# First column kept raw and gated during the forward half; last products of a column scan in two widths, last column stored in four pieces

## The reference

```
x = x + conv0(_gn(x));  x = x + conv1(_gn(x));  x = x + conv2(_gn(x))
# layer 3, on v = _gn(x), column by column (Wc is 1024 x 1024):
def step(prev, x_i):
    y = einsum('oc,nch->noh', Wc, prev) + conv_b
    y = where(y >= 0, y, prelu_a * y)
    return y + x_i
fl  = scan(step, v[..., 0], v[..., 1:])      # forward
out = scan(step, fl[31], fl[30 .. 0])        # back; the last column stays
x = x + out
```

## Time and profile before

| | us |
|---|---|
| median of 3 runs | 910.0 (908.2 to 911.15) |
| the profiled execution | 909.22 |
| its span, first to last instruction | 907.5 |
| TensorE busy | 780.0 (86%) |
| VectorE busy | 688.7 (76%) |
| ScalarE busy | 433.8 (48%) |
| GpSimd busy | 36.3 (4%) |
| mean granted TensorE clock | 0.958 of full |

### The profile page before, as it was taken

One profiled execution on the slowest core, in us unless ns is written; L12 is line 12 of the kernel. 1 busy time (PEld: TensorE's weight loads), 2 busy tenths in 40 slices (PEclk: granted clock), 3 DMA queues, 4 the chain that ended last, 5 costly groups with the idle time before them and its releaser, 6 DMA issues.

```text
span 907.5 us, 12847 instructions
## 1 busy us (share of the span) xinstructions
PE 780.0 (86%) x3604; PEld 629.9 (69%) x3604; DVE 688.7 (76%) x1410; ACT 433.8 (48%) x1380; POOL 36.3 (4%) x68
## 2 busy tenths in 40 slices
PE   0022336999999999999999999999999999999996
PEld 0021224888888888888888888888888888888885
DVE  7977668666766776667766777888888887888887
ACT  6974441444444444444444444444444444444444
POOL 2003420000000000000000000000000000000002
PEclk9996556999999999999999999999999999999998
DMA  8930020000000000000000013332223333332223
GB/s 350 420 159 0 0 94 23 1 1 0 0 0 0 0 0 0 0 0 0 0 0 0 0 46 92 92 92 81 70 80 92 92 92 92 92 92 74 72 85 116
DMA packets 71513, 56.79 MB, mean 63 GB/s; under 512 B 1872, under 2 KB 67408, under 8 KB 69456
## 3 DMA queue, kind: packets, MB, share of 16 engines
q1 hardware_dynamic: 71072, 56.63, 18.8%
q10 hardware_dynamic: 432, 0.07, 0.0%
HBM read 39.91 MB, written 16.78 MB: 62 GB/s over the span
## 4 chain that ended last, share of the span: by engine, by line
PE 85%; DVE 12%; issue 1%; ACT 1%; DMA 1%; ACTq 0%; DVEq 0%
PE ps_prods L530 25%; PE ps_prods L534 25%; PE ps_prods L533 25%; PE ps_turns L542 6%; DVE half_max L610 4%; DVE below_flags L662 2%; PE ps_values L501 2%; DVE bn_parts L605 2%; DMA x_sb<-x_cols 1%; DVE under L668 0%; DVE x_sb L760 0%; PE ps_second L483 0%; PE ps_group L480 0%; DVE t L593 0%; DVE rstd L594 0%
## 5 line engine op out<-in xcount | busy, mean ns | idle before, releaser
L530 PE MATMUL ps_prods<-w_hi,s_hi 128*128 128x512 f32 x992 | 402.2, 405 | 0.3 <-DVE s_lo L750 0.3
L533 PE MATMUL ps_prods<-w_lo,s_hi 128*128 128x512 f32 x992 | 401.4, 405 | 0.0
L534 PE MATMUL ps_prods<-w_hi,s_lo 128*128 128x512 f32 x992 | 391.2, 394 | 0.0
L456 ACT ACTIVATE act_buf<-ps_prods 128x256 f32<-128x256 f32 x248 | 81.9, 382 | 358.8 <-PE ps_prods L534 355.8
L760 DVE SCALAR_TENSOR_TENSOR x_sb<-act_buf,x_sb 128x256 f32 (+1 forms) x248 | 107.3, 433 | 156.3 <-ACT act_buf L462 145.7
L530 PEld LDWEIGHTS ps_prods<-w_hi,s_hi 128*128 128x128 f32 x992 | 186.9, 188 | 39.1 <-DVE s_lo L750 1.1
L534 PEld LDWEIGHTS ps_prods<-w_hi,s_lo 128*128 128x128 f32 x992 | 187.2, 189 | 38.4
L533 PEld LDWEIGHTS ps_prods<-w_lo,s_hi 128*128 128x128 f32 x992 | 187.6, 189 | 32.8
L462 ACT ACTIVATE act_buf<-ps_turns,bias 128x128 f32<-128x128 f32 x496 | 157.6, 377 | 50.8 <-PE ps_turns L542 50.8
L468 ACT ACTIVATE ps_below<-ps_turns,neg_bias 128x128 f32<-128x128 f32 x496 | 153.0, 363 | 0.0
L767 DVE SCALAR_TENSOR_TENSOR x_sb<-ps_below,neg_slope,x_sb 128x256 f32 (+1 forms) x248 | 119.3, 481 | 4.9
(11 more groups left out here) (116 smaller groups left out, 321.3 us busy)
## 6 DMA issues: line engine op xcount, KB each, us to landing
x_sb<-x_cols SPq DMA_DIRECT2D x16, 1024.0 KB, 21.3
stage<-x_cols SPq DMA_DIRECT2D x31, 512.0 KB, 4.1
out_cols<-x_sb SPq DMA_DIRECT2D x31, 512.0 KB, 4.8
w_raw<-w_t SPq DMA_DIRECT2D x8, 512.0 KB, 21.5
x_sb<-x_cols SPq DMA_DIRECT2D x1, 2048.0 KB, 7.9
x_sb<-x_cols SPq DMA_DIRECT2D x1, 512.0 KB, 4.0
out_cols<-x_sb SPq DMA_DIRECT2D x2, 256.0 KB, 2.3
params<-gates ACTq DMA_DIRECT2D x1, 60.0 KB, 5.3
```

The source lines that it names most:

```text
L456: act.activation(act_buf[:, half], ps_prod[c][:, half], ACT.Copy).then_inc(raw_copied, 1)
L530: pe.matmul(ps_prod[c], s_hi[:, k, :], w_hi[:, k, w_cols], start=(k == 0), stop=False)
L533: pe.matmul(ps_prod[c], s_hi[:, k, :], w_lo[:, k, w_cols], start=False, stop=False)
L534: return pe.matmul(ps_prod[c], s_lo[:, k, :], w_hi[:, k, w_cols], start=False, stop=(k == CT - 1))
```

## The change

Four edits go together.

1. The first column is no longer normed in place. VectorE writes its normed pairs to `stage`, which is free then, and splits them from there; column 0 of `x_sb` stays raw. `stage` is loaded with raw x of column 31 once the fourth pair is split (`state_ready` 4), no longer once the last median is spread.
2. The first forward step and the norm of column 2 are taken out of VectorE's loop. Behind them VectorE adds `g_scale + a_scale` and `g_shift + a_shift` and applies both to column 0. The column then holds norm and gated x together, and nothing has to be added to it behind the last step. GpSimd's two operations, SyncE's load of `spare_col` and the two L789 are gone.
3. The last step of TensorE and ScalarE is taken out of their loops. The second half's product is made in two parts of 256 columns, the first before, the second behind the turns of the first half. The second part goes to the bank of the first half, which is free by then. ScalarE copies and biases each part by itself.
4. Column 0 is stored in four pieces of two tiles, each when its sum is done.

```diff
+        both_scale = sb("both_scale", [P, N, CT])
+        both_shift = sb("both_shift", [P, N, CT])
...
-            sp.wait_ge(median_spread, LAYERS)
+            sp.wait_ge(state_ready, 4)
             sp.dma_start(stage_col, x_cols[:, :, COLS - 1, :]).then_inc(x_again, 16)
...
-            sp.wait_ge(out_stored, (COLS - 2) * 16)
-            sp.dma_start(spare_col, x_cols[:, :, 0, :]).then_inc(x_again, 16)
             sp.wait_ge(out_ready, COLS - 1)
             sp.dma_start(out_cols[1].rearrange("p (c m) -> p c m", c=CT), column(1)).then_inc(out_stored, 16)
-            for c in range(2):
-                half = slice(4 * c, 4 * c + 4)
-                sp.wait_ge(out_ready, COLS + c)
-                sp.dma_start(out_cols[0].rearrange("p (c m) -> p c m", c=CT)[:, half, :], column(0, 4 * c, 4))\
+            for q in range(4):
+                pair = slice(2 * q, 2 * q + 2)
+                sp.wait_ge(column_added, (STEPS - 1) * 4 + q + 5)
+                sp.dma_start(out_cols[0].rearrange("p (c m) -> p c m", c=CT)[:, pair, :], column(0, 2 * q, 2))\
                     .then_inc(out_stored, 16)
...
-            pool.wait_ge(gates_folded, 1)
-            pool.wait_ge(x_again, COLS * 16)
-            pool.tensor_tensor(by_image(spare_col), by_image(spare_col), over_rows(a_scale), ALU.mult)\
-                .then_inc(spare_scaled, 1)
-            pool.wait_ge(spare_scaled, 1)
-            pool.tensor_tensor(by_image(spare_col), by_image(spare_col), over_rows(a_shift), ALU.add)\
-                .then_inc(spare_ready, 1)
...
+            with act.Fori(0, STEPS - 1) as i:
...
+            final = STEPS - 1
+            act.wait_ge(product_done, final * 2 + 1)
+            for r in range(2):
+                copy_raw(final, 0, r)
+            for r in range(2):
+                biased_sides(final, 0, r)
+            for r in range(2):
+                act.wait_ge(product_done, final * 2 + 2 + r)
+                copy_raw(final, 1, r, bank=1 - r)
+                biased_sides(final, 1, r)
...
+            def unit_products(c, k, between=None, part=None):
+
+                cols = slice(0, HALF) if part is None else slice(part * 256, part * 256 + 256)
+                out = ps_prod[0 if part else c][:, cols]
...
+                for k in range(2):
+                    unit_products(1, k, part=0)
+                for k in range(4, CT):
+                    if k % 2 == 0:
+                        pe.wait_ge(state_ready, i * 4 + (k // 2 + 1))
+                    last = unit_products(0, k)
+                last.then_inc(product_done, 1)
+                for k in range(2, CT):
+                    last = unit_products(1, k, part=0)
+                last.then_inc(product_done, 1)
+                turn(0, i * 4 + 1)
+                turn(1, i * 4 + 2)
+                for k in range(CT):
+                    last = unit_products(1, k, part=1)
+                last.then_inc(product_done, 1)
+                for r in range(2):
+                    turn(r, i * 4 + 3 + r)
...
-                pair = by_image(column(0, 2 * q, 2))
+                pair = stage_col[:, 2 * q:2 * q + 2, :]
...
+            dve.wait_ge(norm_ready, 1)
+            scan_step(0, 1)
+            norm_column(2, 1)
+
+            dve.tensor_tensor(both_scale[:, :, :], g_scale[:, :, :], a_scale[:, :, :], ALU.add)
+            link(dve.tensor_tensor(both_shift[:, :, :], g_shift[:, :, :], a_shift[:, :, :], ALU.add))
+            dve.tensor_tensor(by_image(column(0)), by_image(column(0)), over_rows(both_scale), ALU.mult)\
+                .then_inc(kept_scaled, 1)
+            dve.wait_ge(kept_scaled, 1)
+            dve.tensor_tensor(by_image(column(0)), by_image(column(0)), over_rows(both_shift), ALU.add)\
+                .then_inc(first_gated, 1)
+            with dve.Fori(1, COLS - 2) as i:
...
+            dve.wait_ge(first_gated, 1)
             scan_step(STEPS - 1, 0, last=True)
```

More of the change, by code:

```diff
@@ L250, in gated_norm_and_column_scan_kernel @@
         stage_col = stage[:, :].rearrange("p (c m) -> p c m", c=CT)
-        spare_col = column(COLS - 1)
         @block.sync
@@ L448, in _, with copy_raw, biased_sides @@
             act.wait_ge(folded, 2)
-            with act.Fori(0, STEPS) as i:
+            def copy_raw(i, c, r, bank=None):
+                half = slice(r * 256, r * 256 + 256)
+                act.wait_ge(column_added, i * 4 + (2 * c + r + 3))
+                act.activation(act_buf[:, half], ps_prod[c if bank is None else bank][:, half], ACT.Copy)                    .then_inc(raw_copied, 1)
+            def biased_sides(i, c, r):
+                act.wait_ge(transposed, i * 4 + (2 * c + r + 1))
+                for j in range(2):
+                    ct = 4 * c + 2 * r + j
+                    last = act.activation(act_buf[:, (2 * r + j) * P:(2 * r + j + 1) * P],
+                                          ps_turn[r][:, j * P:(j + 1) * P], ACT.Identity,
+                                          bias=bias[:, ct:ct + 1])
+                last.then_inc(biased, 1)
+                for j in range(2):
+                    ct = 4 * c + 2 * r + j
+                    last = act.activation(ps_below[:, r * 512 + j * P:r * 512 + (j + 1) * P],
+                                          ps_turn[r][:, j * P:(j + 1) * P], ACT.Relu,
+                                          bias=neg_bias[:, ct:ct + 1], scale=-1.0)
+                last.then_inc(negated, 1)
+            with act.Fori(0, STEPS - 1) as i:
                 for c in range(2):
@@ L567, in scan_step, with final_step @@
                 last.then_inc(product_done, 1)
+            def final_step(i):
+                for k in range(4):
+                    if k % 2 == 0:
+                        pe.wait_ge(state_ready, i * 4 + (k // 2 + 1))
+                    if k == 1:
+                        unit_products(0, k, lambda: turn(0, i * 4 - 1))
+                        turn(1, i * 4)
+                    else:
+                        unit_products(0, k)
+                for k in range(2):
+                    unit_products(1, k, part=0)
+                for k in range(4, CT):
+                    if k % 2 == 0:
+                        pe.wait_ge(state_ready, i * 4 + (k // 2 + 1))
+                    last = unit_products(0, k)
[10 more added lines that the diff above has]
+                    turn(r, i * 4 + 3 + r)
             scan_step(0, True)
             scan_step(1, False)
-            with pe.Fori(2, STEPS, 2) as i:
+            with pe.Fori(2, STEPS - 2, 2) as i:
                 scan_step(i, False)
                 scan_step(i + 1, False)
-            for r in range(2):
-                turn(r, 4 * STEPS - 1 + r)
+            scan_step(STEPS - 2, False)
+            final_step(STEPS - 1)
         @block.vector
@@ L776, in scan_step @@
                             dve.wait_ge(a_state_read, i + 1)
-                        state_high(w, 4 * c, nth)
-                        state_low(w, 4 * c, nth)
+                        state_high(column(w, 4 * c, 2), 4 * c, nth)
+                        state_low(column(w, 4 * c, 2), 4 * c, nth)
                     add_below(1)
                     if not last:
-                        state_high(w, 4 * c + 2, nth + 1)
-                        state_low(w, 4 * c + 2, nth + 1)
-                    else:
-                        half = slice(4 * c, 4 * c + 4)
-                        col = column(w, 4 * c, 4)
-                        dve.wait_ge(column_added, nth + 1)
-                        dve.wait_ge(spare_ready, 1)
-                        dve.tensor_tensor(col, col, spare_col[:, half, :], ALU.add).then_inc(out_ready, 1)
+                        state_high(column(w, 4 * c + 2, 2), 4 * c + 2, nth + 1)
+                        state_low(column(w, 4 * c + 2, 2), 4 * c + 2, nth + 1)
             def gated_column(nth):
```

53 lines of the change are left out of this document (18 added, 35 removed).

## The result

| | before | changed |
|---|---|---|
| median of 22 runs each, us | 910.03 | 908.70 |
| the profiled execution | 909.22 | 908.42 |
| span | 907.5 | 906.6 |

The ratio is 0.9987, 95% interval 0.9981 to 0.9993: 1.3 us faster, where 1.2 us and 908.8 us were forecast. It is clear of no change, and within the 0.3% called "same".

The account below looks back on a forecast made before the run. TensorE was taken to bound the kernel from 153 to 898 us, then the tail behind its last matmul. Tail -1.87 us and stall +0.7 us gave -1.2 us, 908.8 us against the median, range 906.6 to 911.8 us.

Parts of the forecast that it names:

- TensorE bounds the scan: From 153 to 898 us TensorE is never short of work; only delays to it or the tail move the end.
- The stall of the forward half: Behind norm_column(2), new VectorE work of 2.81 us stalls TensorE once, 0.7 us (bounds 0 and 1.1).
- 0.32 us slack: Forward half: first pair usable from 176.32 us, TensorE came for it at 176.64, so 0.32 us of lateness is absorbed.
- GpSimd's contention: Tail: beside GpSimd's operations L804 took 2.82 us and L760 2.20; without them both quick, counted only within the walk.
- The walk through the last step: Last step and tail, operation by operation: last product at 899.28 us, VectorE's end at 903.34, a gain of 1.37 us.
- The narrow matmul: Last step's 256-column matmuls: 0.12 us each, bounds 0.11 and 0.232 us.
- The last store: End of the tail: 128 KB instead of 256 lands 0.5 us sooner, bounds 0 and 0.6.
- tail -1.87 forecast: Last step and tail together: 1.37 us from VectorE's earlier end plus 0.5 us from the smaller last store.
- Halving the columns did halve the time: Rival at the last step's 48 narrow products: halving doesn't halve; at 0.19 us each, 911.8 us; chance 0.13.
- The stall came: Against the rival of no forward-half stall and narrow matmuls at 0.11 us: net -2.3 us, 907.7 us; chance 0.12.
- didn't return each step: Against the rival that VectorE's forward loop refetches instructions each turn: 8 us and up, 918 us; chance 0.02.
- the tail did gain: Against the rival that the last quarter's copy waits longer and the tail gains nothing: -0.5 us, 909.5 us; chance 0.15.

Follow-up runs that it names:

- e4: Changed kernel with the forward work on column 0 put in two places, behind the norms of columns 1 and 2; 906.60 us, ratio 0.9979.
- e8: The changed kernel once more, without any edit, for its profile alone; 907.77 us, one run.
- e2: Kernel before without GpSimd's two operations on the reloaded column 0 (output differs in the last column), L789 kept; 907.52 us, ratio 0.9984.
- e7: Changed kernel with the last step's second 256-column part made as two times 128 columns; 911.18 us, one run.
- e1: Changed kernel, but the last step keeps its full-width product (512 columns) and old order; 907.45 us, ratio 0.9984.
- e5: Changed kernel with column 0's gating in two places and TensorE's last step reordered, six more narrow products first and earlier turns; 906.18 us, ratio 0.9973.
- e3: Kernel before with only the two-part product of the last step added, GpSimd, VectorE and stores as before; 910.23 us, ratio 1.0013.

## Why the prediction was right

- **TensorE bounds the scan:** right. Between the first product and the last step it waits in no step but the second and third of the changed kernel.
- **The stall of the forward half, 0.7 us:** the mechanism was right (e4), the size was half. The first addition was late by 0.80 us against the step's first matmul where the sum had 1.10 us by ends. And the state was late by only 0.63 us: it stood 11.65 us behind its step's first matmul before (176.26 - 164.61) and 12.28 us now (175.58 - 163.30). A late VectorE no longer waits for ScalarE between the first quarter's additions and the second's (their first operations start 0.85 us apart, before 1.03 us), which gave back some 0.17 us. With 0.32 us slack, 0.3 us was left; the next interval adds 0.1 us, and e8 has 0.4 us in all. The term was 0.3 us too large. The slack of 0.32 us held. The sign that the prediction had named for it, 0.5 to 0.8 us of idle time on step 2's first matmul, didn't appear: it was 0.27 us.
- **GpSimd's contention:** the step had named it and left it without a sum of its own. e2 gives it: 1.28 us. The walk had it right implicitly, since it set L804's end at 895.9 in before's time.
- **The walk through the last step:** right to within 0.1 us at each point. From the step's first matmul, forecast and measured: tile 4 at 4.31 and 4.30; the last product's end at 12.58 and 12.62; the last copy at 14.01 and 14.05; VectorE's end at 16.64 and 16.69. The narrow matmul, taken as 0.12 us, took 0.119 us; its lower bound, 0.11 us, turned up at 128 columns (e7).
- **The last store:** 0.5 us was taken, it was 0.41 us (2.79 - 2.38); the landing fell from 2.3 to 2.0 us.
- **The sum:** tail -1.87 forecast, -1.73 measured (20.80 - 19.07); stall +0.7 forecast, +0.4 measured; together -1.2 and -1.3 us. The tail gave 0.14 us less than forecast and the stall cost 0.3 us less; the errors have opposite sign, which flatters the sum a little. That the medians give the same -1.33 us is in part luck, since the interval of their ratio leaves 0.6 to 1.7 us. The two profiled spans differ by 0.9 us, and that is no test of the sum: in front of the scan the changed kernel's execution is 1.5 us earlier, its first step takes 0.2 us more and the 57 steps of the slower pace (e8) 1.7 us more, beside the stall of 0.4 and the tail's -1.7 us.
- **The rivals.** Halving the columns did halve the time (0.119 against 0.232 us). The rule of the Trainium skill ("TensorE: Matmul & The Clock Gate", section "Back-to-back issue gap": 109 ns for 256 columns), which that section gives for an isolated matmul, is 10 ns short, as it was 16 ns short at 512. The stall came, but didn't return each step, and the tail did gain.
- **What the prediction missed** is not in its sum: it walked the two parts only together with GpSimd's leaving, and didn't walk the full-width step without GpSimd. Its own rows would have given that: a last product at 12.0 and a chain of some 4 us, 16.0 us against 16.64. That is what e1 shows.

Open: why the steps of some executions take 12.06 us and of others 12.03, on one kernel. In the profiles of the changed kernel and of e2 the slower pace is even over all steps from the fourth on, with most matmul starts 0.229 or 0.237 us apart where the others have mostly 0.230 to 0.233. In e1, e5 and e7 it sets in on the way: the steps vary between 12.02 and 12.07 us, and the last twenty or so take 12.07 us each. Nor was it tried what sets the 1.3 us in front of the scan.

## What to carry to other kernels

Where two engines share work near the end, first price each edit alone on the same walk: here one edit (GpSimd out of the tail) gave 1.3 us, and another, made together with it, took 0.7 us back until its order was changed. Splitting the last product paid here only where its first part's outcome reached the next engine while the second part was still computed, and only down to the width at which halving still halved a matmul's time. Work moved into an engine's idle time is free only if each piece fits its gap: 2.8 us in a gap of 1.7 us stalled the bound engine, the same work as 1.6 and 1.25 us in two gaps did not.

## What the runs showed of the hardware that was not expected

- A matmul with its own 128x128 weight load costs 0.232 us at 512 columns, 0.119 at 256 and 0.11 at 128 (granted clock 1.00): the time halves once and then hardly falls.
- Beside GpSimd's operations on 128x1024, VectorE's of the same size took 2.82 us for 1.23, and one of a quarter of the size 2.20 us for 0.42. Twice (before and e3) the figures were the same to 0.01 us, and without GpSimd (e2) both were gone. The small operation lost as much as the large one because both ended behind GpSimd's: L375 ended at 893.50 + 2.86 = 896.36 and L804 at 897.45, 1.09 us later; L378, the row below, ended at 899.28 and L760 at 899.56, 0.28 us later. In e3 it is again 1.09 and 0.28 us. That is each time 0.14 us less than VectorE's operation takes alone (1.23 and 0.42 us), as if it had run almost whole behind GpSimd's, whatever its size (GpSimd's rows are rough, and how the one holds the other up isn't shown).

```profile
896.44 2.84 POOL L378 TENSOR_TENSOR x_sb<-x_sb,a_shift 128x1024 f32<-128x1024 f32 x1
```

- TensorE's granted clock was 0.50 from 903 us on in e3, when it had made only one turn since its last product; the last turn, still on the path, took 0.69 us for 0.44 and came 0.25 us later for it. In the profiles before and of the changed kernel the clock was 0.50 from 903 us on too, but their last turns, at 901.40 and 902.04, were over.
